# Two small fp32 matmuls per image split into column halves, and fewer small VectorE operations

## The chip, the cores and the metric

One core of a Trainium2 chip runs the kernel. The metric is the time of one execution on the device in microseconds (us), the median of the runs shown.

## What is computed

The input `x` is 16 images of 32 channels and 96 x 96 points in fp32. Each channel of each image is normalised by itself (32 groups of one channel), then goes through two 3 x 3 convolutions whose kernels are mixed for each image out of seven experts:

```
n      = (x - mean) / sqrt(var + 1e-5)                 per image and channel
pooled = n.mean over the image
gate   = softmax(pooled @ gate_w.T + gate_b)           7 numbers per image
kw1, kb1 = gate-weighted experts + conv1;  kw2, kb2 = the same for conv2
out1   = relu(conv3x3(n, kw1) + kb1)
out2   = conv3x3(out1, kw2) + kb2
result = x + (n + out2)
```

## The kernel before, in words

**Layout.** The 128 partitions hold 4 neighbouring image rows x 32 channels; 24 such bands (25 for the hidden image, which is shifted by one row) lie along the free dimension. A matmul contracts over all 128 partitions (4 rows x 32 channels) and gives 64 columns (2 output rows x 32 channels), for one of three horizontal taps. Rows 1 and 2 of four come from the tile itself ("straight": `a1`, `a2`), the other two from a copy whose partition halves are exchanged and shifted ("crossed": `c1`, `c2`). So each tap is a pair of 128*64 matmuls, one side to PSUM partitions 0 to 63, the other to 64 to 127 (L376). fp16 high and low parts of image and kernel are multiplied in three products; a convolution is 5 groups of 9 pairs, and an image is 90 pairs.

**The order of work.** Every engine runs a list written out by hand, `slot(s)`, for s = 1, 2, ... In slot s TensorE does conv1 of image s and conv2 of image s-1, with two small fp32 matmuls for image s+2 between the groups: `gather_rows` (L359) sums the channel statistics over the four partitions of a channel, `logits` (L367) sums the gate's products over the partitions. Both were one matmul over 128 columns. VectorE does in slot s: the statistics of image s+2 (L601) and `aggregate` (L606 to L608), which prepares the operand of `gather_rows`; `channel_moments` (L616 to L619), which reads the result; the seven steps of `mixture` for image s+1 (L646); `biases` (L656, L657) and `weights` (L663); the low part of the hidden image, `hidden_low` (L677); the rim of the hidden image, `clear_rim` (L684); and `finish` (L693). GpSimd turns the variance into the coefficients (`coefficients`, L846 to L856), forms the low part of the next image (L865) and adds the residual (`residual`, L879). ScalarE normalises (L491, L496), evacuates conv1 (L534), rounds the kernels (L519), copies `a2` into `c2` (`cross2`, L550) and takes exponentials. SyncE's queue loads images (L260), stores results (L274), and makes the crossed copies of the image (L287) and of the kernels (`cross_weights`, L296).

**What ties them together.** conv1 of image s+1 begins with a wait for that image's crossed kernels (`w_crossed`), so after `weights`. VectorE's `channel_moments` stands ahead of six of the seven `mixture` steps and waits for `gather_rows`, which TensorE issues after the fourth group of conv1. `biases` stands ahead of `weights`.

**The rim.** The hidden image needs zero rows above and below. `clear_rim` was called twice per image, after groups 0 and 4 (partitions 64 to 95 of band 0, partitions 96 to 127 of band 24), each with a wait for the low part just written; `cross2` waits for the first of the two before its second half, conv2 for both.

Of the kernel before, what the change touches and what calls it, by code (L numbers as in the profile page):

```python
# [29 lines left out]
F32 = mybir.dt.float32  # L30
# [5 lines left out]
P = 128  # L36
EPS = 1e-5

WS = 16.0
# [51 lines left out]
def build(nc, x, w1, b1, w2, b2, ew1, eb1, ew2, eb2, gw, gb, out):  # L91
# [18 lines left out]
    with ctx:  # L110
# [27 lines left out]
        row = sb("row", [P, 2, G])  # L138
# [3 lines left out]
        minus_half = sb("minus_half", [P, 1])  # L142

# [7 lines left out]
        NUMBER, VEPS, NMEAN, RSTD, NBIAS, RS1, RB, B1, POOLED, NMAX, ESUM, RSUM, MEAN, VAR, SCALED, B2 = range(16)  # L151
# [168 lines left out]
        def _(pe):  # L320
# [35 lines left out]
            def gather_rows(t):  # L356

                pe.wait_ge(mv_ok, t.number + 1)
                nc.tensor.matmul(pstat[:, 0:3 * G], same[:, :],  # L359
                                 triples[t.parity][:, :, :].rearrange("p g a -> p (g a)"),  # L360
                                 start=True, stop=True).then_inc(rows_ps, 1)

            def logits(t):
                pe.wait_ge(gwp_ok, t.number + 1)
                if not t.known(0):
                    pe.wait_ge(logit_ok, t.number)
                nc.tensor.matmul(pgate[:, 0:E], ones[:, :], gwp[t.ring][:, :],  # L367
                                 start=True, stop=True).then_inc(gate_ps, 1)
# [48 lines left out]
            def conv2_group(s, g):  # L417
                if g == 0:

                    pe.wait_ge(lo2_ok, (s.number + 1) * GRP)  # L420
                    pe.wait_ge(crossed2, s.number + 1)
                    pe.wait_ge(rim_ok, 2 * (s.number + 1))

                if s.at_least(N - 1):
                    pe.wait_ge(fin_ok, (s.number - 1) * GRP + g + 1)
                else:
                    pe.wait_ge(hid_ok, (s.number + 1) * GRP + g + 1)
                n = min(SPG, NB - g * SPG)
                products(1, s, g, PRODUCTS,
                      (CROSSED, c2[s.parity], g * SPG, n, 0),  # L430
                      (STRAIGHT, a2[s.parity], g * SPG + 1, n, 0)).then_inc(conv2_ps, 1)
# [36 lines left out]
        def _(act):  # L468
# [70 lines left out]
            def cross2(t, half):  # L539


                if half == 1:
                    act.wait_ge(rim_ok, 2 * t.number + 1)
                else:
                    act.wait_ge(lo2_ok, (t.number + 1) * GRP)
                    if t.at_least(2):
                        act.wait_ge(conv2_ps, (t.number - 1) * GRP)
                d, a = (halves(k[t.parity])[half].rearrange("p a b w -> p a (b w)").bitcast(F32) for k in (c2, a2))
                first = (1 - half) * RP // 2
                last = nc.scalar.copy(d, a[:, :, first:first + NB * RP // 2])  # L550
                if half == 1:
                    last.then_inc(crossed2, 1)
# [34 lines left out]
        def _(dve):  # L587
# [16 lines left out]
            def aggregate(t):  # L604

                link(nc.vector.bn_aggr(mv[t.ring][:, :], stats[t.ring][:, :, :].rearrange("p a b -> p (a b)")))  # L606
                nc.vector.tensor_scalar(triples[t.parity][:, :, 1], row[:, 0, :], mv[t.ring][:, 0:1], None, ALU.mult)
                nc.vector.tensor_scalar(triples[t.parity][:, :, 2], row[:, 1, :], mv[t.ring][:, 1:2], None,  # L608
                                        ALU.mult).then_inc(mv_ok, 1)

            def channel_moments(t):
# [4 lines left out]
                nc.vector.tensor_copy(c[:, NUMBER:NUMBER + 1], pstat[:, 0:1])  # L616
                link(nc.vector.bn_aggr(c[:, MEAN:VAR + 1], pstat[:, 0:3 * G]))
                nc.vector.tensor_scalar(c[:, NMEAN:NMEAN + 1], c[:, MEAN:MEAN + 1], -1.0, None, ALU.mult)
# [32 lines left out]
            def biases(t):  # L651
# [3 lines left out]
                mixed = mix[:, E % 2, :, TAPS:TAPS + 1]  # L655
                nc.vector.tensor_scalar(c[:, B1:B1 + 1], mixed[:, 0, :], HS / WS, None, ALU.mult)  # L656
                nc.vector.tensor_scalar(c[:, B2:B2 + 1], mixed[:, 1, :], 1.0 / WS, None, ALU.mult).then_inc(bias_ok, 1)  # L657
# [22 lines left out]
            def clear_rim(s, g):  # L680

                dve.wait_ge(lo2_ok, s.number * GRP + g + 1)
                p0, j = (P - 2 * C, 0) if g == 0 else (P - C, NS - 1)
                nc.vector.memset(a2[s.parity][p0:p0 + C, :, j, 1:1 + W], 0.0).then_inc(rim_ok, 1)  # L684
# [26 lines left out]
            def row_constants():  # L711
# [5 lines left out]
                link(nc.vector.tensor_reduce(row[:, 0, :], ident[:, :].rearrange("p (g c) -> p g c", g=G), AX_X, ALU.add))  # L717
                link(nc.vector.tensor_scalar(row[:, 1, :], row[:, 0, :], float(PIX), None, ALU.mult))
                for i in range(2):
                    last = nc.vector.tensor_copy(triples[i][:, :, 0], row[:, 1, :])  # L720
# [58 lines left out]
            clear_rim(Sample(0, 0), 0)  # L779
# [4 lines left out]
            clear_rim(Sample(0, 0), GRP - 1)  # L784
# [3 lines left out]
            def slot(s):  # L788
# [4 lines left out]
                run(clear_rim, s, 0, 0, 0)  # L793
# [15 lines left out]
                run(clear_rim, s, 0, 0, GRP - 1)  # L809
# [10 lines left out]
        def _(pool):  # L820
            link = Link(pool, pool_link)
            nc.gpsimd.memset(minus_half[:, :], -0.5)

# [12 lines left out]

            for straight, shifted in ((a1, c1), (a2, a2)):
# [5 lines left out]
            def coefficients(t):  # L843
# [3 lines left out]
                nc.gpsimd.tensor_tensor(c[:, NBIAS:NBIAS + 1], c[:, NMEAN:NMEAN + 1], c[:, RSTD:RSTD + 1],  # L847
                                        ALU.mult).then_inc(coef_ok, 1)
# [70 lines left out]
```

## Time and profile before

| | |
|---|---|
| median of 3 runs | 365.44 us (365.11 to 365.81) |
| the profiled execution | 366.37 us, of which the span of the trace is 364.6 us |
| busy: PE, VectorE, ScalarE, GpSimd | 317.4, 288.0, 252.8, 192.9 us |

The span runs from the first to the last instruction of the trace; the time of an execution includes some microseconds around it. Busy shares are averages over the start (until about 69 us), the steady slots (to about 303 us) and the end, in which only TensorE has much to do.

### The profile page before, as it was taken

How to read it: one execution, taken by the hardware profiler on the slowest of the kernel's cores; microseconds unless marked ns; L12 is line 12 of the kernel's file. 1: busy time of each engine (PE TensorE's matmuls, PEld its weight loads, DVE VectorE, ACT ScalarE, POOL GpSimd, SP SyncE). 2: the span in 40 equal slices, each digit the busy share in tenths (PEclk: the TensorE clock that was granted, in tenths of full speed). 3: DMA queues.
4: the chain of work that ended last, by engine and by line, in shares of the span. 5: the costliest groups of instructions: out<-in, count | busy, mean ns of one | idle time of the engine just before them, and what ended most of it. 6: DMA issues, size and time to landing. Idle time of an engine off the chain costs nothing.

```text
span 364.6 us, 7708 instructions
## 1 busy us (share of the span) xinstructions
PE 317.4 (87%) x2983; PEld 200.6 (55%) x2983; DVE 288.0 (79%) x651; ACT 252.8 (69%) x278; POOL 192.9 (53%) x236
## 2 busy tenths in 40 slices
PE   2327664499999999999899989999999999999994
PEld 2216432257565656565566646575756565676552
DVE  4699945698989989898979896989989898693432
ACT  1155219896878778787869695878887797965710
POOL 8039517492838475665739391848475656921000
PEclk9999989599999999999999999999999999999999
DMA  9932930599989797989997899979898977575055
GB/s 197 222 70 57 227 77 3 120 167 202 210 186 211 177 216 179 211 174 205 191 217 145 201 199 220 173 180 219 186 211 188 211 173 151 122 174 142 0 131 130
DMA packets 109379, 60.86 MB, mean 167 GB/s; under 512 B 102944, under 2 KB 105248, under 8 KB 109344
## 3 DMA queue, kind: packets, MB, share of 16 engines
q1 hardware_dynamic: 108544, 59.79, 78.9%
q10 hardware_dynamic: 608, 0.59, 0.6%
q8 instruction: 23, 0.38, 0.5%
q14 instruction: 12, 0.10, 0.1%
q0 software_dynamic: 192, 0.01, 0.0%
HBM read 19.47 MB, written 18.87 MB: 105 GB/s over the span
## 4 chain that ended last, share of the span: by engine, by line
PE 60%; DVE 19%; DMA 10%; SPq 3%; ACT 3%; POOL 2%; issue 2%; ACTq 0%; DVEq 0%; POOLq 0%
PE pg L376 56%; DVE mix L646 9%; DMA wts<-wts 7%; DVE a L677 3%; DVE wts L663 3%; DMA c<-a 2%; PE pg L339 2%; DVE stats L601 2%; PE pstat L359 2%; POOL a L865 1%; SPq L260 1%; DMA natural<-in_L_conv_conv_w 1%; SPq L296 1%; SPq L287 1%; ACT xh L491 1%
## 5 line engine op out<-in xcount | busy, mean ns | idle before, releaser
L376 PE MATMUL pg<-a,wts 128*64 128x480 f16 (+1 forms) x1440 | 292.2, 362 | 11.3 <-DMA c<-a 6.3
L376 PE MATMUL pg<-c,wts 128*64 128x480 f16 (+1 forms) x1440 | 297.7, 366 | 0.0
L376 PEld LDWEIGHTS pg<-c,wts 128*64 128x64 f16 x1440 | 154.5, 110 | 72.2 <-issue 1.1
L376 PEld LDWEIGHTS pg<-a,wts 128*64 128x64 f16 x1440 | 154.8, 110 | 43.3 <-issue 8.7
L865 POOL TENSOR_TENSOR a<-xh,a 128x576 f16<-128x576 f32 x64 | 79.1, 1268 | 13.4 <-POOL col L873 9.3
L534 ACT ACTIVATE hid<-pg,col 128x480 f32<-128x480 f32 x80 | 52.5, 657 | 46.7 <-PE pg L376 37.1
L646 DVE SCALAR_TENSOR_TENSOR mix<-bank,gate,mix 128x386 f32<-128x386 f32 x96 | 73.9, 770 | 2.4
L846 POOL TENSOR_TENSOR col<-col,minus_half 128x1 f32<-128x1 f32 x16 | 13.5, 841 | 111.6 <-DVE col L619 111.6
L550 ACT COPY c<-a 64x2352 f32<-64x2352 f32 x32 | 68.9, 2152 | 2.1 <-DVE a L677 1.9
L677 DVE TENSOR_TENSOR a<-hid,a 128x480 f16<-128x480 f32 x80 | 52.5, 657 | 21.2 <-ACT a L534 20.9
L693 DVE SCALAR_TENSOR_TENSOR img<-pg,img 128x480 f32<-128x480 f32 (+1 forms) x80 | 48.2, 632 | 13.6 <-PE pg L376 13.1
L879 POOL TENSOR_SCALAR img<-img,col 128x1152 f32<-128x1152 f32 x32 | 57.9, 1817 | 0.1
L534 ACT ACTIVATE a<-pg,col 128x480 f16<-128x480 f32 x80 | 52.5, 656 | 0.0
L601 DVE BATCH_NORM_STATS2 stats<-img 128x6 f32<-128x384 f32 x96 | 45.6, 544 | 0.1
L491 ACT ACTIVATE xh<-img,col 128x2304 f32<-128x2304 f32 x16 | 36.9, 2306 | 11.3 <-POOL col L847 11.3
L496 ACT ACTIVATE a<-img,col 128x2304 f16<-128x2304 f32 (+1 forms) x17 | 37.3, 2194 | 6.5 <-POOL col L847 6.5
L663 DVE TENSOR_TENSOR wts<-mix,wts 128x384 f16<-128x384 f32 x16 | 20.6, 1288 | 0.3 <-ACT wts L519 0.3
L359 PE MATMUL pstat<-triples,same 128*128 128x12 f32 x32 | 7.0, 293 | 15.4 <-DVE triples L608 15.4
L519 ACT CAST wts<-mix 128x384 f16<-128x384 f32 x16 | 8.2, 512 | 15.9 <-DVE mix L646 15.9
L359 PEld LDWEIGHTS pstat<-triples,same 128*128 128x128 f32 x32 | 5.5, 215 | 21.4 <-DVE triples L608 16.0
L616 DVE COPY col<-pstat 128x1 f32<-128x1 f32 x16 | 2.5, 157 | 18.6 <-PE pstat L359 18.6
L339 PE MATMUL pg<-ident,padded 128*128 128x128 f32 x24 | 5.6, 424 | 8.4 <-DVE padded L707 8.4
(61 smaller groups left out, 143.4 us busy)
## 6 DMA issues: line engine op xcount, KB each, us to landing
c<-a SPq DMA_DIRECT2D x28, 588.0 KB, 7.0
img<-in_x SPq DMA_DIRECT2D x56, 288.0 KB, 7.0
out<-img SPq DMA_DIRECT2D x60, 180.0 KB, 3.0
out<-img SPq DMA_DIRECT2D x60, 108.0 KB, 2.6
wts<-wts SPq DMA_DIRECT2D x28, 96.0 KB, 2.5
c<-a SPq DMA_DIRECT2D x8, 294.0 KB, 5.9
img<-in_x SPq DMA_DIRECT2D x16, 144.0 KB, 5.0
out<-img SPq DMA_DIRECT2D x4, 120.0 KB, 2.1
```

The costliest lines, as they stand in the source:

```text
L376: last = nc.tensor.matmul(pg[g][side * 64:side * 64 + 64, at:at + nb * W].rearrange("p (b w) -> p b w", w=W), wts[s.c % WSETS][kind][:, v, ...
L491: nc.scalar.activation(xh[t.parity][:, :, :], img[t.ring][:, :, :], ACT.Identity, bias=c[:, NBIAS:NBIAS + 1], scale=c[:, RSTD:RSTD + 1]).t ...
L496: return nc.scalar.activation(a1[t.parity][:, HI, b0:b1, 1:1 + W], img[t.ring][:, b0:b1, :], ACT.Identity, bias=c[:, NBIAS:NBIAS + 1], sca ...
L534: last = nc.scalar.activation(o, pg[g][:, 0:SPG * W].rearrange("p (b w) -> p b w", w=W), ACT.Relu, bias=c[:, B1:B1 + 1], scale=HS / WS)
L550: last = nc.scalar.copy(d, a[:, :, first:first + NB * RP // 2])
L601: last = nc.vector.bn_stats(stats[t.ring][:, j, :], flat[:, j * SC:(j + 1) * SC])
L646: nc.vector.scalar_tensor_tensor(out=mix[:, (e + 1) % 2, :, :], in0=bank[:, e, :, :], scalar=gate[t.ring][:, e:e + 1], in1=bank[:, E, :, : ...
L663: nc.vector.tensor_tensor(st[:, :, LO, :], mix[:, E % 2, :, 0:TAPS], st[:, :, HI, :], ALU.subtract).then_inc(w_ok, 1)
L677: nc.vector.tensor_tensor(a2[s.parity][:, LO, j0:j1, 1:1 + W], hid[g_parity(s, g)][:, :, :], a2[s.parity][:, HI, j0:j1, 1:1 + W], ALU.subt ...
L693: nc.vector.scalar_tensor_tensor(out=r, in0=pg[g][:, 0:(b1 - b0) * W].rearrange("p (b w) -> p b w", w=W), scalar=1.0 / (WS * HS), in1=r, o ...
L865: last = nc.gpsimd.tensor_tensor(a1[t.parity][:, LO, b0:b1, 1:1 + W], xh[t.parity][:, b0:b1, :], a1[t.parity][:, HI, b0:b1, 1:1 + W], ALU. ...
L879: last = nc.gpsimd.tensor_scalar(img[t.ring][:, b0:b1, :], img[t.ring][:, b0:b1, :], c[:, RS1:RS1 + 1], c[:, RB:RB + 1], ALU.mult, ALU.add)
```

## The change

1. `gather_rows` and `logits` issue two fp32 matmuls of 64 columns each in place of one of 128 columns. The semaphore is raised by the second.
2. `aggregate`: one `tensor_tensor` with a broadcast pair in place of two `tensor_scalar`.
3. `channel_moments`: a copy of a number that nothing reads (L616) and the negated mean (L618) are gone; GpSimd negates in the instruction that forms the bias of the normalisation.
4. `biases`: one `tensor_tensor` with a constant pair in place of two `tensor_scalar`.
5. `clear_rim` is called once per image. The zero row of band 0 is written into both `c2` buffers once at the start by GpSimd, and `cross2` leaves that piece alone, which makes three copies of two.

```
-                nc.tensor.matmul(pstat[:, 0:3 * G], same[:, :],
-                                 triples[t.parity][:, :, :].rearrange("p g a -> p (g a)"),
-                                 start=True, stop=True).then_inc(rows_ps, 1)
+                for h0, h1 in ((0, P // 2), (P // 2, P)):
+                    last = nc.tensor.matmul(pstat[h0:h1, 0:3 * G], same[:, h0:h1],
+                                            triples[t.parity][:, :, :].rearrange("p g a -> p (g a)"),
+                                            start=True, stop=True)
+                last.then_inc(rows_ps, 1)
...
-                nc.tensor.matmul(pgate[:, 0:E], ones[:, :], gwp[t.ring][:, :],
-                                 start=True, stop=True).then_inc(gate_ps, 1)
+                for h0, h1 in ((0, P // 2), (P // 2, P)):
+                    last = nc.tensor.matmul(pgate[h0:h1, 0:E], ones[:, h0:h1], gwp[t.ring][:, :],
+                                            start=True, stop=True)
+                last.then_inc(gate_ps, 1)
...
-                    pe.wait_ge(rim_ok, 2 * (s.number + 1))
+                    pe.wait_ge(rim_ok, s.number + 1)
...
-                if half == 1:
-                    act.wait_ge(rim_ok, 2 * t.number + 1)
-                else:
+                def copy(p0, p1, b0, b1, first):
+                    d, a = (k[t.parity][p0:p1, :, :, :].rearrange("p a b w -> p a (b w)").bitcast(F32) for k in (c2, a2))
+                    r = RP // 2
+                    return nc.scalar.copy(d[:, :, b0 * r:b1 * r], a[:, :, (b0 + first) * r:(b1 + first) * r])
+                if half == 0:
                     act.wait_ge(lo2_ok, (t.number + 1) * GRP)
...
+                    copy(0, P // 2, 0, NB, 1)
+                else:
+                    copy(P - C, P, 0, 1, 0)
+                    copy(P // 2, P, 1, NB, 0).then_inc(crossed2, 1)
...
-                nc.vector.tensor_scalar(triples[t.parity][:, :, 1], row[:, 0, :], mv[t.ring][:, 0:1], None, ALU.mult)
-                nc.vector.tensor_scalar(triples[t.parity][:, :, 2], row[:, 1, :], mv[t.ring][:, 1:2], None,
-                                        ALU.mult).then_inc(mv_ok, 1)
+                pair = mv[t.ring][:, :].rearrange("p (o a) -> p o a", o=1).to_broadcast([P, G, 2])
+                nc.vector.tensor_tensor(triples[t.parity][:, :, 1:3], row[:, :, :], pair, ALU.mult).then_inc(mv_ok, 1)
...
-                nc.vector.tensor_copy(c[:, NUMBER:NUMBER + 1], pstat[:, 0:1])
                 link(nc.vector.bn_aggr(c[:, MEAN:VAR + 1], pstat[:, 0:3 * G]))
-                nc.vector.tensor_scalar(c[:, NMEAN:NMEAN + 1], c[:, MEAN:MEAN + 1], -1.0, None, ALU.mult)
...
-                mixed = mix[:, E % 2, :, TAPS:TAPS + 1]
-                nc.vector.tensor_scalar(c[:, B1:B1 + 1], mixed[:, 0, :], HS / WS, None, ALU.mult)
-                nc.vector.tensor_scalar(c[:, B2:B2 + 1], mixed[:, 1, :], 1.0 / WS, None, ALU.mult).then_inc(bias_ok, 1)
+                nc.vector.tensor_tensor(c[:, B1:B2 + 1], mix[:, E % 2, :, TAPS], bias_scales[:, :],
+                                        ALU.mult).then_inc(bias_ok, 1)
...
-            def clear_rim(s, g):
+            def clear_rim(s):
-                dve.wait_ge(lo2_ok, s.number * GRP + g + 1)
-                p0, j = (P - 2 * C, 0) if g == 0 else (P - C, NS - 1)
-                nc.vector.memset(a2[s.parity][p0:p0 + C, :, j, 1:1 + W], 0.0).then_inc(rim_ok, 1)
+                dve.wait_ge(lo2_ok, (s.number + 1) * GRP)
+                nc.vector.memset(a2[s.parity][P - C:P, :, NS - 1, 1:1 + W], 0.0).then_inc(rim_ok, 1)
...
+            nc.gpsimd.memset(bias_scales[:, 0:1], HS / WS)
+            nc.gpsimd.memset(bias_scales[:, 1:2], 1.0 / WS)
...
+            pool.wait_ge(ident_ok, 1)
+            for i in range(2):
+                link(nc.gpsimd.memset(c2[i][P // 2:P - C, :, 0, :], 0.0))
...
-                nc.gpsimd.tensor_tensor(c[:, NBIAS:NBIAS + 1], c[:, NMEAN:NMEAN + 1], c[:, RSTD:RSTD + 1],
-                                        ALU.mult).then_inc(coef_ok, 1)
+                nc.gpsimd.tensor_scalar(c[:, NBIAS:NBIAS + 1], c[:, MEAN:MEAN + 1], c[:, RSTD:RSTD + 1], -1.0,
+                                        ALU.mult, ALU.mult).then_inc(coef_ok, 1)
```

How this stands in the order of VectorE's instructions, in a steady slot from the low part of group 0 to the moments of the channels, before:

```order
L677 TENSOR_TENSOR a_0<-hid,a_0 128x5x96
L606 BN_AGGR mv<-stats 128x2
L607 TENSOR_SCALAR triples<-row,mv 128x4
L608 TENSOR_SCALAR triples<-row,mv 128x4
L684 MEMSET a_0 32x2x96
L635 RECIPROCAL col<-col 128x1
L636 TENSOR_SCALAR gate<-expo,col 128x7
L646 SCALAR_TENSOR_TENSOR mix<-bank,gate 128x386
L677 TENSOR_TENSOR a_0<-hid,a_0 128x5x96
L616 COPY col<-pstat 128x1
L617 BN_AGGR col<-pstat 128x2
L618 TENSOR_SCALAR col<-col 128x1
```

and now (the lines are those of the changed file):

```order
L679 TENSOR_TENSOR a_0<-hid,a_0 128x5x96
L612 BN_AGGR mv<-stats 128x2
L614 TENSOR_TENSOR triples<-row,mv 128x4x2
L638 RECIPROCAL col<-col 128x1
L639 TENSOR_SCALAR gate<-expo,col 128x7
L649 SCALAR_TENSOR_TENSOR mix<-bank,gate 128x386
L679 TENSOR_TENSOR a_0<-hid,a_0 128x5x96
L621 BN_AGGR col<-pstat 128x2
L622 TENSOR_SCALAR col<-col 128x1
```

Four instructions are gone from this stretch (one of the pair that fills `triples`, the first memset, the copy and the negation); a fifth goes later in the slot, where `biases` stands.

ScalarE's order at the end of a slot, where `c2` is made, before:

```order
L519 CAST wts_0<-mix 128x2x192
L496 ACTIVATE a_1<-img,col 128x24x96
L550 COPY c_1<-a_1 64x2352 x2
L510 ACTIVATE expo,col<-logit,col 128x7
L534 ACTIVATE hid<-pg,col 128x480
```

and now:

```order
L549 COPY c_1<-a_1 64x2352
L549 COPY c_1<-a_1 32x2x49
L549 COPY c_1<-a_1 64x2x1127
L515 ACTIVATE expo,col<-logit,col 128x7
L539 ACTIVATE hid<-pg,col 128x480
```

The second copy has become a small one (32 partitions, one band) and one over 23 bands in place of 24.

## Rows read from the trace of the kernel before

**Rows 1.** The page: busy time, share of the span, instructions
```profile
PE 317.4 (87%) x2983; PEld 200.6 (55%) x2983; DVE 288.0 (79%) x651; ACT 252.8 (69%) x278; POOL 192.9 (53%) x236
```
**Rows 2.** Timeline, PE: the gathers (start us, us); intervals of slots, and one wait
```profile
89.56 0.39 PE L359 MATMUL pstat<-triples,same 128*128 128x12 f32 x2
...
187.09 0.39 PE L359 MATMUL pstat<-triples,same 128*128 128x12 f32 x2
...
205.97 0.39 PE L359 MATMUL pstat<-triples,same 128*128 128x12 f32 x2
...
302.96 0.39 PE L359 MATMUL pstat<-triples,same 128*128 128x12 f32 x2
```
**Rows 3.** Waits: waiter <- waited for: us in total, times, longest us
```profile
PEld pg L376 <- DMA wts<-wts: 7.3, 8, 2.2
PEld pgate L367 <- issue: 5.4, 14, 0.4
PEld pstat L359 <- issue: 5.4, 13, 0.8
```
**Rows 4.** Timeline, PE and PEld around one gather
```profile
166.26 0.57 PE L376 MATMUL pg<-c,wts 128*64 128x480 f16 x2
166.76 0.39 PE L359 MATMUL pstat<-triples,same 128*128 128x12 f32 x2
...
167.08 0.39 PE L376 MATMUL pg<-c,wts 128*64 128x480 f16 x1
...
166.76 0.30 PEld L359 LDWEIGHTS pstat<-triples,same 128*128 128x128 f32 x2 [0.39 <-issue]
```
**Rows 5.** Chain of waits, 160 to 180 us: start us, us, what
```profile
174.91 0.52 SPq L296
...
175.47 4.11 DMA wts<-wts
```
**Rows 6.** Timeline, VectorE, same slot
```profile
163.60 0.23 DVE L607 TENSOR_SCALAR triples<-row,mv 128x4 f32<-128x4 f32 x1
...
164.30 0.16 DVE L635 RECIPROCAL col<-col 128x1 f32<-128x1 f32 x1
...
167.19 0.16 DVE L616 COPY col<-pstat 128x1 f32<-128x1 f32 x1 [1.23 <-PE pstat L359]
167.26 0.20 DVE L617 BATCH_NORM_AGGREGATE col<-pstat 128x2 f32<-128x12 f32 x1
167.50 0.15 DVE L618 TENSOR_SCALAR col<-col 128x1 f32<-128x1 f32 x1
167.57 0.14 DVE L619 TENSOR_SCALAR col<-col 128x1 f32<-128x1 f32 x1
...
173.37 0.14 DVE L657 TENSOR_SCALAR col<-mix 128x1 f32<-128x1 f32 x1
173.43 1.45 DVE L663 TENSOR_TENSOR wts<-mix,wts 128x384 f16<-128x384 f32 x1
```
**Rows 7.** Timeline, GpSimd; L663 and L296: duration ns min/median/max; landings
```profile
170.71 3.77 POOL L879 TENSOR_SCALAR img<-img,col 128x1152 f32<-128x1152 f32 x2
L663 DVE TENSOR_TENSOR wts<-mix,wts x16: 548/1450/1452, 29.8 to 325.9; 128x384 f16<-128x384 f32 x16
DMA to landing us min/median/max: 2.1/2.5/4.6
```
**Rows 8.** Busy by stretches: length, PE, PEld, DVE, ACT, POOL; clock, DMA share, GB/s
```profile
187.20:206.00 18.80, 18.80 (x185) 11.85 (x185) 17.25 (x39) 15.60 (x17) 11.74 (x13) 1.00 0.84 179
206.00:226.90 20.90, 19.10 (x186) 11.87 (x185) 17.24 (x39) 15.60 (x17) 11.75 (x13) 1.00 1.01 208
```
**Rows 9.** Chain of waits, start of the kernel
```profile
53.63 0.22 DVE a L684
...
61.34 2.03 ACT c L550
```
**Rows 10.** Groups by line: busy us, mean ns of one | idle before
```profile
L510 ACT ACTIVATE expo<-logit,col 128x7 f32<-128x7 f32 x16 | 4.8, 300 | 2.1 <-DVE col L628 1.8
```

More of the change, by code:

```diff
@@ L137, in build @@
         same = sb("same", [P, P])
-        row = sb("row", [P, 2, G])
+        row = sb("row", [P, G, 2])
         triples = [sb(f"triples{i}", [P, G, 3]) for i in range(2)]
@@ L142, in build @@
         minus_half = sb("minus_half", [P, 1])
+        bias_scales = sb("bias_scales", [P, 2])
         stats = [sb(f"stats{i}", [P, STAT, 6]) for i in range(RING)]
@@ L150, in build @@
         gate = [sb(f"gate{i}", [P, E]) for i in range(RING)]
-        NUMBER, VEPS, NMEAN, RSTD, NBIAS, RS1, RB, B1, POOLED, NMAX, ESUM, RSUM, MEAN, VAR, SCALED, B2 = range(16)
+        VEPS, RSTD, NBIAS, RS1, RB, B1, B2, POOLED, NMAX, ESUM, RSUM, MEAN, VAR, SCALED = range(14)
         pg = [ctx.enter_context(nc.psum_tensor(f"pg{i}", [P, 512], F32)) for i in range(GRP)]
@@ L547, in cross2 @@
                         act.wait_ge(conv2_ps, (t.number - 1) * GRP)
[L548 to L552, printed above, removed]
+                    copy(0, P // 2, 0, NB, 1)
+                else:
+                    copy(P - C, P, 0, 1, 0)
+                    copy(P // 2, P, 1, NB, 0).then_inc(crossed2, 1)
             load_kernels()
@@ L716, in row_constants @@
                     nc.vector.tensor_copy(same[:, g * C:(g + 1) * C], pick[:, :])
-                link(nc.vector.tensor_reduce(row[:, 0, :], ident[:, :].rearrange("p (g c) -> p g c", g=G), AX_X, ALU.add))
-                link(nc.vector.tensor_scalar(row[:, 1, :], row[:, 0, :], float(PIX), None, ALU.mult))
+                link(nc.vector.tensor_reduce(row[:, :, 0], ident[:, :].rearrange("p (g c) -> p g c", g=G), AX_X, ALU.add))
+                link(nc.vector.tensor_scalar(row[:, :, 1], row[:, :, 0], float(PIX), None, ALU.mult))
                 for i in range(2):
-                    last = nc.vector.tensor_copy(triples[i][:, :, 0], row[:, 1, :])
+                    last = nc.vector.tensor_copy(triples[i][:, :, 0], row[:, :, 1])
                 link(last)
@@ L778, in _ @@
             channel_moments(Sample(0, 2))
-            clear_rim(Sample(0, 0), 0)
             hidden_low(Sample(0, 0), 1)
@@ L783, in _ @@
             hidden_low(Sample(0, 0), 4)
-            clear_rim(Sample(0, 0), GRP - 1)
+            clear_rim(Sample(0, 0))
             statistics(Sample(0, 3))
@@ L792, in slot @@
                 run(aggregate, s, 2, 2)
-                run(clear_rim, s, 0, 0, 0)
                 run(softmax_out, s, 1, 1)
@@ L808, in slot @@
                 run(hidden_low, s, 0, 0, 4)
-                run(clear_rim, s, 0, 0, GRP - 1)
+                run(clear_rim, s, 0, 0)
                 run(finish, s, -1, 0, 0)
```

## The prediction

> **What bounds the kernel now.** I read the page first: TensorE is busy 87% of the span, VectorE 79% [rows 1]. Neither share says what the next microsecond waits for, so I then took the timeline of TensorE and measured from one `gather_rows` to the next. The 11 intervals from 89.56 to 302.96 us make 213.4 us, 19.40 on average [rows 2]. Four of them are 18.9, such as 187.09 to 205.97 [rows 2]: that is TensorE with nothing to wait for. Eleven of these would be 207.7, so 5.7 us are waits. The list of waits names them: the weight loads of L376 wait 7.3 us in 8 places for the crossed kernels' DMA [rows 3].
>
> So two loops of nearly one length bound a slot, and the longer one wins:
> - **TensorE's own work**, 18.88 us.
> - **The loop of the kernels**: gather, VectorE's moments, six mixture steps, `biases`, `weights`, the DMA, conv1 of the next image, the next gather. In the slot shown the gather starts at 166.76 [rows 4], VectorE goes on at 167.19 [rows 6], SyncE issues the crossing at 174.91, its second DMA starts at 175.47 and takes 4.11 [rows 5]; conv1 begins and its next gather starts at 187.09 [rows 2]. Without the DMA d that is 187.09 - 166.76 - 4.11 = 16.22. The loop is 16.22 + d and wins if d is over 2.66. The landings are 2.1 at least, 2.5 in the middle, 4.6 at most [rows 7], which is why some slots wait and others don't.
>
> **The split matmuls.** Around a gather the last convolution matmul starts at about 166.46 (two starts in 0.57 us, each some 0.37 long) [rows 4]. Pairs follow each other every 0.204 us, so the next was due at 166.66; it starts at 167.08 [rows 4]. One small fp32 matmul thus costs TensorE 0.42 us: 0.10 before it starts (its load has 0.39 idle before it [rows 4], and both kinds together 10.8 us in 27 places [rows 3]) and 0.32 for two passes about 0.11 apart and the restart. It is the only instruction in the stream that takes 128 columns. Once it has the width of its neighbours, I expect the pause ahead of it to go. Against this stand four passes in place of two. Upper bound of a gain: passes of half the width take half of 0.11 and the two halves run side by side as the convolution's sides do, 0.11 in all, gain 0.31. Lower bound: four full passes (0.44), the pause (0.10) and the restart (0.10) stay, 0.64, a loss of 0.22. I take a cost of 0.17 and a gain of **0.25**, nearer the upper end, since rows 4 show two 64-column matmuls of the convolution going without any pause. Two per slot: 0.50.
>
> The Trainium skill (TensorEngine Tiling (Array Packing), Key Properties) says that changing the tiling mode drains the engine; the 0.39 idle is consistent with it. The same page (Instruction Overhead) gives a matmul some 60 cycles however short it is, which speaks against more passes: an estimate from it is 25 ns for each of four passes, 0.10 in all, and a gain of 0.32, 0.14 more per slot than the 0.50 that the sum takes. No row here shows that floor.
>
> **VectorE, on the loop.** Gone are L616 and L618. From the starts, L616 to L617 is 0.07 and L618 to L619 0.07 [rows 6]; together 0.14. `biases` becomes one instruction, worth 0.06 (L657 to L663 [rows 6]). But L663 takes 1.45 here and 0.55 at its fastest [rows 7], beside GpSimd's residual, which runs from 170.71 for 3.77 us [rows 7]: VectorE's instruction with two tensor inputs seems to wait for GpSimd. The new `biases` also has two tensor inputs and stands right ahead of it; it may wait in its place, and then the 0.06 is lost, and another 0.07 with it. I take 0 (between -0.07 and +0.06). GpSimd's new two-step negation: between 0 and 0.05 (one step of `tensor_scalar` against `tensor_tensor` there), beside VectorE's mixture; I take 0. The result reaches VectorE 0.43 after the gather's start; with the pause gone but more passes behind, between 0.1 sooner and 0.2 later; I take 0. The loop becomes 16.08 + d.
>
> **VectorE, off the loop.** From L607 to L635 there are 0.70 us [rows 6]: three instructions and a wait, where one stays. That gains 0.35 to 0.5 of VectorE's time, but VectorE then waits 1.23 for the gather [rows 6]. In steady slots it is worth nothing.
>
> **ScalarE** gets a third copy: at most the 0.30 of its smallest instruction [rows 10], less 0.08 for the shorter one. It is busy 15.6 of 18.8 us [rows 8] and conv2 needs `c2` some 9 us after it is made; hidden. GpSimd's two memsets at the start run while it waits for VectorE: nothing.
>
> **The sum**, against the profiled execution's 366.37 us:
> - Start, before 69 us: no slot runs yet and VectorE is in the chain. The pairs and the copies save about 0.4 ahead of image 0's low part; L616, L618 and the memset with its wait (0.07 + 0.07 + 0.33, of which the memset's 0.22 stands in the chain [rows 9]) save 0.47; the next `aggregate` 0.13; the added copy takes back 0.2, since L550 is in the chain here [rows 9]. **-0.8**.
> - First full slot, bound by TensorE: **-0.5**.
> - Four free intervals fall from 18.88 to the longer of 18.38 and 16.08 + 2.4: about 0.4 each, **-1.6**.
> - Seven waiting intervals gain what the loop gains, 0.14, a little more where the longer pause lets the loads drain: 0.15 each, **-1.05**.
> - End: one gather and one `logits` of TensorE's own work: **-0.4**.
>
> Together -4.35, so 362.0 for that execution. It lies 0.93 above the median of the runs (365.44), so the prediction for the median is **361.1**.
>
> **The rivals.**
> 1. *The DMA takes it back.* In the slot with the long crossing the DMA engines are busy for all of it (share 1.01), in the free one 0.84 [rows 8]. Shorter slots leave less room, and d could grow by what TensorE gains; or the split buys nothing because the pause stays. Then the start, the end and a little remain: 365.44 - 0.8 - 0.5 - 7 x 0.1 = 363.4. Against it: loads and crossing keep their distance, since both follow TensorE.
> 2. *Slower: the split costs more than it saves.* Place: between group 3 of conv1 and group 4, and in conv2. At the lower bound each call costs 0.22 more: 4 x 0.44 in free slots, 7 x (0.22 + 0.22 later result - 0.14) in waiting ones, 0.44 + 0.44 at the ends, less 0.8: +3.9, so 369.0. It decides from about 0.08 more per call.
> 3. *Slower: the new `biases` queues behind GpSimd by itself*, and L663 again: another 0.9 (1.45 - 0.55) in the loop, less 0.14; free slots have 0.26 to spare. About 11 x 0.55 less 1.7, +4: 369.8. The Trainium skill (GPSIMD Engine Reference, Key points) says that the two engines contend when VectorE has two SBUF inputs. Against it: GpSimd's residual has two parts only, and one mixture step and L663 already take one each.
> 4. *Much better.* `biases` in its one step gets in ahead of GpSimd's second part, or the crossing lands within 2.3 us in most slots. Then all slots are TensorE's 18.38: 213.4 - 202.2 = 11.2 less, with start and ends 1.7: 352.5. A part of it, 357, is likelier.
>
> **Chances.** Forecast 0.57 (its own range 359.5 to 362.8, from a gain of 0.17 to 0.31 per split and the bounds above); rival 1 0.20; rival 4 0.12; rivals 2 and 3 0.11 together. The range 357.0 to 364.6 leaves out rivals 2 and 3 and half of 4. A measurement of this kernel tells 0.2% (0.7 us) from no change: faster 0.84, same 0.06, slower 0.10.
>
> **What the profile after would show.** PEld's "issue" idle before the two small matmuls (10.8 us) gone; a free interval of about 18.4; VectorE 0.07 earlier at each removed instruction; L616 and L618 gone, and the waits for the crossed kernels in more slots, since TensorE's part of the race shrank more than the loop's. I am wrong if the small matmuls still have a pause before them, if the free interval is not under 18.7, or if the new `biases` takes about 1 us and L663 still 1.4.

## The result, and the profile after

The changed kernel took 358.4 us in the median of four runs (357.09 to 359.55), where 361.1 was predicted; the ratio to the kernel before is 0.9753 (95% interval 0.971 to 0.9795). It is faster, as forecast, but by 2.5% where 1.2% was expected. Here and below a ratio is taken over the executions within 1.5% of a kernel's fastest, a median over all of them. The profiled execution took 357.09 us, its span is 355.1 us, 9.5 less than before. The page of the changed kernel, first part:

```profile
PE 308.5 (87%) x3047; PEld 218.8 (62%) x3047; DVE 269.6 (76%) x571; ACT 254.0 (72%) x294; POOL 204.7 (58%) x240
```

These answer to [rows 1]. GpSimd is 12 us busier although it got only four memsets at the start (240 instructions in place of 236) and the negation inside an instruction that it already had; that is the first sign of what the prediction missed.

**Slots.** The changed kernel's timeline of TensorE, the two halves of a gather, at three successive slots (columns: start us, us):

```profile
105.68 0.23 PE L361 MATMUL pstat<-triples,same 128*64 128x12 f32 x2
106.04 0.23 PE L361 MATMUL pstat<-triples,same 128*64 128x12 f32 x2
...
123.49 0.23 PE L361 MATMUL pstat<-triples,same 128*64 128x12 f32 x2
124.22 0.23 PE L361 MATMUL pstat<-triples,same 128*64 128x12 f32 x2
...
143.35 0.23 PE L361 MATMUL pstat<-triples,same 128*64 128x12 f32 x2
143.72 0.23 PE L361 MATMUL pstat<-triples,same 128*64 128x12 f32 x2
```

The later half marks the slot, since the result is complete with it: 106.04, 124.22, 143.72, so 18.18 us for a free slot (18.88 before, 18.38 forecast) and 19.50 for one that waits. From the gather that was at 89.56 before to the last [rows 2], 11 intervals now make 294.15 - 87.02 = 207.13 us, 6.3 less than the 213.4 of before; 11 free ones would be 200.0, so 7.1 us are waits, more than the 5.7 of before.

**Around the small matmul.** The same timeline at the second of these gathers, PE:

```profile
123.41 0.36 PE L381 MATMUL pg<-c,wts 128*64 128x480 f16 x1
123.49 0.23 PE L361 MATMUL pstat<-triples,same 128*64 128x12 f32 x2
123.61 0.57 PE L381 MATMUL pg<-c,wts 128*64 128x480 f16 x2
123.82 0.39 PE L381 MATMUL pg<-a,wts 128*64 128x480 f16 x1
...
124.22 0.23 PE L361 MATMUL pstat<-triples,same 128*64 128x12 f32 x2
...
124.31 0.37 PE L381 MATMUL pg<-c,wts 128*64 128x480 f16 x1
```

The rows before showed a standstill of 0.42 us [rows 4]. Now one half goes at 123.49, while the other side of the array still works on the convolution, and the second half 0.73 us later. The two sides do not stop together as before. By the difference of the free slots, (18.88 - 18.18) / 2, a small matmul costs 0.35 less than the 0.42 of before, so some 0.07 us. The timeline has 0.09 for the side of the second half (`c`, from 124.22 to 124.31). The side of the first half goes on only 0.33 after it, at 123.82, and the slot is a free one all the same; what that side waits for isn't shown.

**Waits** of the changed kernel that answer to [rows 3] (us in total, times, longest):

```profile
DVE col L621 <- PE pstat L361: 22.2, 14, 4.0
PEld pg L381 <- DMA wts<-wts: 8.5, 7, 2.0
PEld pstat L361 <- issue: 0.2, 1, 0.2
```

Of the 10.8 us of "issue" before the small matmuls 0.2 are left. The first line is VectorE waiting for the gathers, 18.6 us before.

**VectorE's stretch of the loop**, the changed kernel's timeline, to be read against [rows 6]:

```profile
124.49 0.22 DVE L621 BATCH_NORM_AGGREGATE col<-pstat 128x2 f32<-128x12 f32 x1 [1.40 <-PE pstat L361]
124.74 0.15 DVE L622 TENSOR_SCALAR col<-col 128x1 f32<-128x1 f32 x1
124.81 1.93 DVE L649 SCALAR_TENSOR_TENSOR mix<-bank,gate,mix 128x386 f32<-128x386 f32 x3
126.66 0.66 DVE L679 TENSOR_TENSOR a<-hid,a 128x480 f16<-128x480 f32 x1
127.22 1.93 DVE L649 SCALAR_TENSOR_TENSOR mix<-bank,gate,mix 128x386 f32<-128x386 f32 x3
129.07 0.65 DVE L679 TENSOR_TENSOR a<-hid,a 128x480 f16<-128x480 f32 x1
129.64 1.10 DVE L658 TENSOR_TENSOR col<-mix,bias_scales 128x2 f32<-128x2 f32 x1
130.66 0.55 DVE L665 TENSOR_TENSOR wts<-mix,wts 128x384 f16<-128x384 f32 x1
```

SyncE issues the crossing at 131.24, 6.75 us after the result is read. Before, it was 174.91 - 167.19 = 7.72 [rows 5, 6]. The stretch is 0.97 shorter, where I had forecast 0.14. `biases` now takes 1.10 us and `weights` only 0.55 (1.45 before [rows 6]), as one of my bounds had it. But the last three mixture steps, 1.93 together, hold no long one any more, and that is new. The kernel before, timeline of VectorE and then of GpSimd, in the slot of [rows 6]:

```profile
170.04 2.77 DVE L646 SCALAR_TENSOR_TENSOR mix<-bank,gate,mix 128x386 f32<-128x386 f32 x3
...
168.93 0.22 POOL L849 TENSOR_SCALAR col<-col 128x1 f32<-128x1 f32 x1
```

GpSimd in the slot shown of the changed kernel:

```profile
124.97 0.88 POOL L850 TENSOR_TENSOR col<-col,minus_half 128x1 f32<-128x1 f32 x1 [5.19 <-DVE col L622]
125.96 0.26 POOL L851 TENSOR_SCALAR col<-col 128x1 f32<-128x1 f32 x1
126.19 0.64 POOL L853 TENSOR_SCALAR col<-col 128x1 f32<-128x1 f32 x1
126.79 0.57 POOL L854 TENSOR_TENSOR col<-mv,col 128x1 f32<-128x1 f32 x1
...
128.55 4.33 POOL L883 TENSOR_SCALAR img<-img,col 128x1152 f32<-128x1152 f32 x2
```

L883, the residual, starts 4.06 us after the moments were begun; before, L879 at 170.71 [rows 7] started 3.45 after L617 at 167.26 [rows 6]. GpSimd is later, and VectorE is faster for it. `hidden_low` (L679) also has two tensor inputs, but keeps its 0.65 us beside the residual (129.07) as elsewhere, so not every such instruction is held.

**The crossing.** The changed kernel's chain of waits in that slot (start us, us, what), against [rows 5]:

```profile
131.24 0.97 SPq L297
132.25 4.05 DMA wts<-wts
136.35 7.18 PE pg L381 x70
```

and its view of line L297:

```profile
DMA to landing us min/median/max: 2.1/3.2/4.9
```

The median time to land went from 2.5 [rows 7] to 3.2 us.

### The profile page after: what moved, and what is told of

The parts are those of the page before. It is cut to its first block, busy times and chain, and to the rows that moved or that the text cites. A ratio compares the mean times of both kernels' runs of the same rounds, so it can differ in the third digit from the quotient of the medians.

```text
span 355.1 us, 7776 instructions
## 1 busy us (share of the span) xinstructions
PE 308.5 (87%) x3047; PEld 218.8 (62%) x3047; DVE 269.6 (76%) x571; ACT 254.0 (72%) x294; POOL 204.7 (58%) x240
## 3 DMA queue, kind: packets, MB, share of 16 engines
HBM read 19.47 MB, written 18.87 MB: 108 GB/s over the span
## 4 chain that ended last, share of the span: by engine, by line
PE 66%; DVE 18%; DMA 8%; ACT 3%; issue 3%; SPq 1%; ACTq 0%; DVEq 0%
PE pg L381 63%; DVE mix L649 7%; DMA wts<-wts 7%; DVE a L679 2%; DVE col L658 2%; PE pg L340 2%; DVE stats L607 2%; DMA natural<-in_L_conv_conv_w 1%; DVE wts L665 1%; SPq L297 1%; DVE wts L672 1%; PE pstat L361 1%; ACT xh L496 1%; ACT c L549 1%; ACT a L501 1%
## 5 line engine op out<-in xcount | busy, mean ns | idle before, releaser
L381 PE MATMUL pg<-a,wts 128*64 128x480 f16 (+1 forms) x1440 | 291.9, 363 | 11.5 <-DMA wts<-wts 6.1
L381 PE MATMUL pg<-c,wts 128*64 128x480 f16 (+1 forms) x1440 | 292.4, 367 | 0.0
L381 PEld LDWEIGHTS pg<-c,wts 128*64 128x64 f16 x1440 | 154.3, 110 | 49.4 <-issue 0.9
L381 PEld LDWEIGHTS pg<-a,wts 128*64 128x64 f16 x1440 | 155.0, 110 | 46.6 <-DMA wts<-wts 8.5
L549 ACT COPY c<-a 64x2352 f32<-64x2352 f32 (+2 forms) x48 | 71.9, 1497 | 2.3 <-DVE a L679 1.9
L679 DVE TENSOR_TENSOR a<-hid,a 128x480 f16<-128x480 f32 x80 | 53.1, 665 | 22.6 <-ACT a L539 22.4
L649 DVE SCALAR_TENSOR_TENSOR mix<-bank,gate,mix 128x386 f32<-128x386 f32 x96 | 62.9, 655 | 2.4
L883 POOL TENSOR_SCALAR img<-img,col 128x1152 f32<-128x1152 f32 x32 | 64.6, 2025 | 0.1
L621 DVE BATCH_NORM_AGGREGATE col<-pstat 128x2 f32<-128x12 f32 x16 | 3.4, 216 | 22.2 <-PE pstat L361 22.2
L361 PE MATMUL pstat<-triples,same 128*64 128x12 f32 x64 | 7.4, 209 | 14.2 <-DVE triples L614 14.2
L361 PEld LDWEIGHTS pstat<-triples,same 128*64 128x64 f32 x64 | 8.1, 154 | 16.4 <-DVE triples L614 14.8
L658 DVE TENSOR_TENSOR col<-mix,bias_scales 128x2 f32<-128x2 f32 x16 | 15.9, 992 | 0.1
L371 PEld LDWEIGHTS pgate<-gwp,ones 128*64 128x64 f32 x64 | 7.9, 144 | 9.3 <-POOL gwp L860 7.4
```

Source lines behind the costliest of these rows:

```text
L381: last = nc.tensor.matmul(pg[g][side * 64:side * 64 + 64, at:at + nb * W].rearrange("p (b w) -> p b w", w=W), wts[s.c % WSETS][kind][:, v, ...
L549: return nc.scalar.copy(d[:, :, b0 * r:b1 * r], a[:, :, (b0 + first) * r:(b1 + first) * r])
L649: nc.vector.scalar_tensor_tensor(out=mix[:, (e + 1) % 2, :, :], in0=bank[:, e, :, :], scalar=gate[t.ring][:, e:e + 1], in1=bank[:, E, :, : ...
L658: nc.vector.tensor_tensor(c[:, B1:B2 + 1], mix[:, E % 2, :, TAPS], bias_scales[:, :], ALU.mult).then_inc(bias_ok, 1)
L679: nc.vector.tensor_tensor(a2[s.parity][:, LO, j0:j1, 1:1 + W], hid[g_parity(s, g)][:, :, :], a2[s.parity][:, HI, j0:j1, 1:1 + W], ALU.subt ...
L883: last = nc.gpsimd.tensor_scalar(img[t.ring][:, b0:b1, :], img[t.ring][:, b0:b1, :], c[:, RS1:RS1 + 1], c[:, RB:RB + 1], ALU.mult, ALU.add)
```

## The experiments

Theory A: the change holds two separate gains, the split (TensorE's own period and an earlier result) and a shift of GpSimd's instructions against VectorE's; the crossing DMA takes part of both back. Theory B: the split is behind all of it. All times below are medians of runs made beside the kernel before on the same chip; "stretch" is the time from the reading of the moments (L617 before, L621 in the changed kernel) to the issue of the crossing, 7.65 in the kernel before, which is the 7.72 less the removed copy's 0.07, and 6.75 in the changed one. The kernel before had a median of 366.9 beside e1 to e4, 367.1 beside e5 to e8 and 368.4 beside e9 to e12; so ratios are compared rather than times.

### One piece again (e1_unsplit)

```diff
-                for h0, h1 in ((0, P // 2), (P // 2, P)):
-                    last = nc.tensor.matmul(pstat[h0:h1, 0:3 * G], same[:, h0:h1], ...
+                nc.tensor.matmul(pstat[:, 0:3 * G], same[:, :], ...
```

and the same in `logits`. Expected:

> The changed kernel with both small fp32 matmuls in one piece of 128 columns again; all else of the change stays. Theory A (two separate gains: the split shortens TensorE's own period and hands the result over earlier, and a shift of GpSimd's work frees VectorE from one of two collisions): VectorE's stretch from the moments of a slot to the issue of the crossing stays at about 6.75 us, a free slot goes back to 18.88 us, few slots wait for the crossed kernels; about 361 us. Theory B (everything comes from the split, the shorter VectorE stretch too): the stretch is 7.6 us again, 364 us.

Measured: 362.2 us, ratio 0.9861 (0.9806 to 0.9916). The stretch is 6.74, 8 of the 11 intervals are 18.87 or 18.88, and TensorE's weight loads wait for the crossing in three places, 2.3 us in all. Theory A holds: the shorter stretch has nothing to do with the split.

### The split alone (e2_split_only)

The kernel before with the split matmuls of the change and nothing else. Expected:

> The kernel before with nothing but the two small matmuls split. Theory A: a free slot takes 18.2 us, the result reaches VectorE 0.25 us earlier, VectorE's stretch stays 7.7 us and more slots wait for the crossing; about 361.5 us. Theory B: the stretch falls to about 6.8 as well and the time is within 1 us of the changed kernel, 358.5 us.

Measured: ten executions spread from 361.1 to 371.9 us, median 367.0 where theory A had 361.5; ratio 0.9886 (0.9835 to 0.9937). The profiled execution took 367.2 us. The stretch is 7.65. Slots of 18.2 to 18.6 us alternate with slots of 19.9 to 22.3. Its waits (same columns as above):

```profile
PEld pg L380 <- DMA wts<-wts: 15.8, 9, 3.0
```

TensorE's own period fell by 0.70 as in the changed kernel, and the wait for the crossing rose from 7.3 [rows 3] to 15.8 us. By itself the split is worth half of the change's gain or nothing. The loop of the kernels has not got shorter with it, so that the wait grows; e3, which has the same stretch and the same waits, agrees. The two slots of over 22 us hold something else besides, TensorE's clock, which is shown under e3.

### The negation back on VectorE (e3_negation_back)

The changed kernel with

```diff
+                nc.vector.tensor_scalar(c[:, NMEAN:NMEAN + 1], c[:, MEAN:MEAN + 1], -1.0, None, ALU.mult)
...
-                nc.gpsimd.tensor_scalar(c[:, NBIAS:NBIAS + 1], c[:, MEAN:MEAN + 1], c[:, RSTD:RSTD + 1], -1.0,
-                                        ALU.mult, ALU.mult).then_inc(coef_ok, 1)
+                nc.gpsimd.tensor_tensor(c[:, NBIAS:NBIAS + 1], c[:, NMEAN:NMEAN + 1], c[:, RSTD:RSTD + 1],
+                                        ALU.mult).then_inc(coef_ok, 1)
```

Expected:

> The changed kernel with the negated mean made by VectorE again and GpSimd's plain product in place of its two-step one. Theory A (GpSimd's instruction after it just misses the boundary between two mixture steps because the two-step form is some 0.05 us longer, and everything behind it on GpSimd shifts by 0.6 us): GpSimd's residual starts 3.1 us after the first mixture step again in place of 3.7, the last mixture step takes 1.4 us again, VectorE's stretch is 7.6 us in place of 6.75; 360.5 us. Rival C (the added instruction costs only its 0.07 us): residual at 3.7, stretch 6.8, 358.6 us.

Measured: ten executions, one of 836.7 us and the others from 363.7 to 372.1, median 368.5; ratio 0.9995 (0.9947 to 1.0043). One instruction of 0.07 us on VectorE, back in its place with the plain product on GpSimd, takes away the whole gain of the change. Timeline of this kernel, VectorE, then GpSimd:

```profile
110.88 2.77 DVE L650 SCALAR_TENSOR_TENSOR mix<-bank,gate,mix 128x386 f32<-128x386 f32 x3
...
114.14 0.15 DVE L659 TENSOR_TENSOR col<-mix,bias_scales 128x2 f32<-128x2 f32 x1
114.23 1.49 DVE L666 TENSOR_TENSOR wts<-mix,wts 128x384 f16<-128x384 f32 x1
```

```profile
109.59 0.20 POOL L852 TENSOR_TENSOR col<-col 128x1 f32<-128x1 f32 x1
109.77 0.22 POOL L854 TENSOR_SCALAR col<-col 128x1 f32<-128x1 f32 x1
109.95 0.49 POOL L855 TENSOR_TENSOR col<-mv,col 128x1 f32<-128x1 f32 x1
...
111.55 3.76 POOL L884 TENSOR_SCALAR img<-img,col 128x1152 f32<-128x1152 f32 x2
```

The moments are read at 108.09, so the residual starts 3.46 after them and the stretch is 7.65, as before the change. The small GpSimd instruction L854 takes 0.22 here and 0.64 in the changed kernel (L853 there). The mixture's steps begin at 108.47 and follow each other by 0.65: here L854 starts at 109.77, 1.30 after the first, at the seam between the second and third step; in the changed kernel it starts 126.19 - 124.81 = 1.38 after, has missed the seam, and lasts until the next one (126.83 against 126.74, the end of the third). What I had put down as "0 to 0.05 us" of GpSimd's new form decides by these hundredths over 0.6 us of GpSimd's time and 0.84 of VectorE's. The pair of `biases` (L659) isn't held here, 0.15 us, and `weights` is, 1.49: which of the two it is also hangs on where GpSimd stands.

The marks of theory A are all there, but its time of 360.5 us isn't. Waits for the crossing are 15.0 us in 8 places, much as in e2, and part of the rest is the clock. Two slots of this kernel by stretches (length, PE, PEld, VectorE, ScalarE, GpSimd busy; clock, DMA share, GB/s):

```profile
165.00:187.50 22.50, 20.06 (x194) 13.89 (x191) 16.79 (x35) 15.80 (x18) 11.75 (x13) 0.92 1.04 216
246.00:266.50 20.50, 18.34 (x192) 14.28 (x190) 16.70 (x35) 15.79 (x18) 11.74 (x13) 1.00 1.02 212
```

In the first, TensorE's granted clock fell from 2.4 to 1.2 GHz (0.51 from 179 us on, 1.00 again by 183) after the weight loads had waited 2.8 us for the crossing, and TensorE is busy 1.7 us longer for about as many matmuls. It happens in two of the five slots with a wait of over 2 us here, and in two of five in e2's profile (the slots of 22.2 and 22.3 us); the longest such wait of the kernel before is 2.2 us [rows 3], and its clock stays at 1.00 through the slots. That the wide spread of e2 and e3 comes from this is likely, but not shown, since one trace of each was kept.

### The negation alone (e4_negation_only)

The kernel before with L618 gone and GpSimd's two-step form, nothing else. Expected:

> The kernel before with nothing but the negation moved into GpSimd's instruction. Theory A: the residual starts at 3.7 us after the first mixture step, the last mixture step takes 0.6 us in place of 1.46, VectorE's stretch is 6.8 us in place of 7.72, nearly all slots run at TensorE's 18.88 us; 361 us. Rival C: only 0.07 us of the stretch goes, 365 us.

Measured: 362.4 us, ratio 0.9857 (0.9802 to 0.9912). Residual 4.05 after the moments, stretch 6.66. This part alone gives about half of the gain (0.0143 of 0.0247, or of the 0.0299 that the changed kernel had when it was run again), as does all of the change without the split (0.9861).

### Work added, nothing removed (e6_small_op_added)

The kernel before with

```diff
+                nc.gpsimd.tensor_scalar(spare[:, :], c[:, RSTD:RSTD + 1], 1.0, None, ALU.add)
                 nc.gpsimd.tensor_scalar(c[:, RS1:RS1 + 1], c[:, RSTD:RSTD + 1], 1.0, None, ALU.add)
```

Expected:

> The kernel before with one more small GpSimd instruction (a 128 x 1 tensor_scalar into a spare tile) in the coefficients of each image; nothing is taken away. Theory A (GpSimd's place among VectorE's instructions decides): what follows misses a boundary of the mixture steps, the residual starts 4.1 us after the moments in place of 3.45, the last mixture step takes 0.6 us in place of 1.46 and the stretch from the moments to the issue of the crossing is 6.8 us in place of 7.65: faster by 3 to 4 us, 362 us, although work was only added. Rival D (the shorter stretch came from the instructions that VectorE no longer has): stretch 7.65, 366 us.

Measured: 361.6 us, ratio 0.9859 (0.9822 to 0.9896). Its GpSimd and its VectorE:

```profile
130.32 0.22 POOL L850 TENSOR_SCALAR spare<-col 128x1 f32<-128x1 f32 x1
130.51 0.51 POOL L851 TENSOR_SCALAR col<-col 128x1 f32<-128x1 f32 x1
...
132.76 4.25 POOL L881 TENSOR_SCALAR img<-img,col 128x1152 f32<-128x1152 f32 x2
```

```profile
131.43 1.93 DVE L647 SCALAR_TENSOR_TENSOR mix<-bank,gate,mix 128x386 f32<-128x386 f32 x3
```

The added instruction takes the seam, the next waits for the following one, the residual starts 4.11 after the moments (128.65), and no mixture step is held. So the gain is not the removed instruction's: 16 needless instructions make the kernel before 1.4% faster.

### `biases` in two instructions again (e7_biases_back)

```diff
-                nc.vector.tensor_tensor(c[:, B1:B2 + 1], mix[:, E % 2, :, TAPS], bias_scales[:, :],
-                                        ALU.mult).then_inc(bias_ok, 1)
+                nc.vector.tensor_scalar(c[:, B1:B1 + 1], mixed[:, 0, :], HS / WS, None, ALU.mult)
+                nc.vector.tensor_scalar(c[:, B2:B2 + 1], mixed[:, 1, :], 1.0 / WS, None, ALU.mult).then_inc(bias_ok, 1)
```

Expected:

> The changed kernel with `biases` as two tensor_scalar again. Theory A: VectorE waits for GpSimd's residual once in either form, at `biases` (1.1 us) with the pair and at `weights` (1.45 us) without; the stretch is 6.75 us within 0.1 and the time that of the changed kernel, 358 us. Rival: the pair of inputs is what costs, and the stretch gets 0.5 us shorter or more, 356 us.

Measured: 356.3 us, ratio 0.9717 (0.9674 to 0.976); the changed kernel has 0.9753 and, run again, 0.9701, so the times do not tell the two apart. The profiles do: the stretch is 6.67 against 6.75 (`weights` takes 1.04 here after 0.25 of waiting for ScalarE, where I had expected 1.45), and at the start of the kernel `biases` of image 0 stands beside GpSimd's low part. Changed kernel, then this one, VectorE:

```profile
28.27 1.25 DVE L658 TENSOR_TENSOR col<-mix,bias_scales 128x2 f32<-128x2 f32 x1
29.45 0.15 DVE L628 SCALAR_TENSOR_TENSOR logit<-pgate,gbias 128x7 f32<-128x7 f32 x1
```

```profile
28.26 0.15 DVE L659 TENSOR_SCALAR col<-mix 128x1 f32<-128x1 f32 x1
28.33 0.14 DVE L660 TENSOR_SCALAR col<-mix 128x1 f32<-128x1 f32 x1
```

The pair takes 1.25 us there, the two single ones 0.29; behind them ScalarE's exponential of image 1 starts at 29.18 in place of 29.83. Whether this edit of the change costs more than it saves these times can't tell; e10 below can.

### The crossed copies by VectorE (e5_copy_on_vector)

The changed kernel without `cross_weights` in SyncE's list and with

```diff
                 run(weights, s, 1, 1)
+                run(cross_early, s, 1, 1)
```

Expected:

> The changed kernel with the crossed copy of each image's kernels made by two VectorE copies right behind `weights` in place of two DMAs. If the DMA's time to land (3 to 5 us in every second slot) is what holds the changed kernel back, the waits for the crossed kernels go and every slot takes TensorE's own 18.2 us: 11 intervals 200 us in place of 207, 351 us. If VectorE, which gains 0.8 to 1.7 us of work per slot on 16.7, becomes the bound, intervals are 18.4 to 19 and the time is 353 to 358. If the DMA was not the brake, 358 us as the changed kernel.

Measured: 359.1 us, ratio 0.9791 (0.9752 to 0.983), no faster than the changed kernel. All waits for the crossing are gone, and 12 others of 0.52 us have come, one in each slot: conv1 waits for `finish` on VectorE. Every interval is 18.9. Over 88 to 288 us VectorE is busy 194 of 200 us: it is the bound now, as the second of the expected cases said, though the time is 1 us above the 353 to 358 of that case.

### The copies shared (e8_copy_shared)

As e5, but ScalarE makes one of the two, behind its high part:

```diff
+                nc.scalar.copy(halves(cr)[1].rearrange("p v a b -> p (v a b)").bitcast(F32),
+                               halves(st)[0].rearrange("p v a b -> p (v a b)").bitcast(F32)).then_inc(w_crossed[t.ring], 16)
```

Expected:

> As the copies by VectorE, but one of the two is made by ScalarE behind its high part of the next image. Both engines have room (ScalarE 16 us of 18.2, VectorE 16.7), and the copies are done some 9.5 us after the gather where conv1 begins at 10.8: all slots 18.2 us, 351 us. If ScalarE's place in the order comes too late, conv1 waits in every slot and intervals are 18.5 to 19: 354 to 358 us.

Measured: 351.1 us, ratio 0.9565 (0.9535 to 0.9595). TensorE, by stretches (length, PE, PEld, VectorE, ScalarE, GpSimd busy; clock, DMA share, GB/s), waits for nothing:

```profile
88.00:180.00 92.00, 92.00 (x958) 65.44 (x954) 85.79 (x178) 80.40 (x96) 63.45 (x65) 1.00 0.94 194
180.00:288.00 108.00, 108.00 (x1120) 75.28 (x1117) 101.46 (x208) 96.06 (x114) 76.17 (x78) 1.00 0.97 200
```

So the crossing DMA took 5 to 7 us back from the change (0.9753 or, run again, 0.9701, less 0.9565, of 366). The DMA engines are as busy as before (0.94 to 0.97); they move images and results in time, and it is only the short transfer that conv1 stood waiting for that held it up.

### Four together (e9 to e12)

The changed kernel again, and three kernels that differ by one part from e8: `biases` in two, the small matmuls in one piece, and the shared copies in the kernel before.

> The changed kernel as it is, beside the three below. 358.4 us as before; stretch 6.75 us, every second slot waiting for the crossed kernels.

Measured: 357.3 us, ratio 0.9701 (0.9664 to 0.9737).

> The kernel with the crossed copies shared by VectorE and ScalarE, and `biases` as two tensor_scalar again. If a slot there is TensorE's own work, the form of `biases` is worth nothing any more: 351 us within 0.7. If VectorE was still close behind, 350 us or less.

Measured: 348.8 us, ratio 0.9471 (0.9435 to 0.9507), the fastest of all and clear of e8. The intervals are those of e8, 18.18; the gain lies at the start, where the moments of image 3 are read at 67.08 us in place of 68.77, with ScalarE's exponential of image 1 0.76 us earlier (29.12 against 29.88), as in e7. The rest of these 1.7 us lies in the wait for the DMA of the crossed image, and no run separates it. In all kernels with the split the moments of images 1 and 2 are 26.2 to 26.8 us apart with `biases` in two (e2, e7, e10) and 27.4 to 27.9 with the pair (the changed kernel, e3, e5, e8, e9). I had looked for a difference in the slots only.

> The shared copies with both small matmuls in one piece again. With no wait for a DMA the slots show the price of the 128-column form alone: 18.88 us in place of 18.18 in every slot, 0.70 x 11 intervals and 1 to 1.4 at the ends over the 351 us of the shared copies, 360 us.

Measured: 360.2 us, ratio 0.9772 (0.9736 to 0.9809). Every interval is 18.87 or 18.88. This is the price of the two 128-column matmuls with nothing else in the way: 0.70 in each of 11 intervals is 7.7 us, and the ratios of e11 and e8 differ by 0.0207 or 7.6 us. Its waits show them as before the change:

```profile
PEld pgate L367 <- issue: 5.4, 14, 0.4
PEld pstat L359 <- issue: 5.4, 13, 0.8
```

> The kernel before with the shared copies and nothing else. If the loop through the crossing DMA was all that held the kernel before over TensorE's 18.88 us, all intervals are 18.88 and 5.7 us go: 361 us. If VectorE, with 0.8 us more work in a slot than the changed kernel has, comes to bound it, intervals are 19 and more, 363 us.

Measured: 360.9 us, ratio 0.9805 (0.9767 to 0.9844), every interval 18.87 or 18.88. Beside e11 it shows that without the DMA in the loop all of the change but the split is worth nothing that these runs can tell (0.9772 and 0.9805, intervals that overlap): a shorter stretch only counts while the crossing is late.

## Why the prediction was right or wrong

**What bounds the kernel: right.** Two loops, TensorE's own work and the loop of the kernels through the crossing; e12 removed the second and all slots fell to 18.88.

**The split: right in kind, gain too small.** I took 0.25 us for each call; measured is (18.88 - 18.18) / 2 = 0.35, above my upper bound of 0.31. The bound assumed that both sides pause together for 0.11. They don't: each side takes its half in its own stream. The pause ahead came from the width, as I had guessed. The Trainium skill (TensorEngine Tiling (Array Packing), Key Properties) says that tiles operate independently and that changing the mode drains the engine; e11 and e8 agree with both, 0.42 against 0.07 us, though a drain as such is seen in no trace. Its 60 cycles for a short matmul (Instruction Overhead) gave an estimate of 0.10 us for four passes, and so 0.05 for the two that each side has; the 0.07 measured lies between.

**The result's latency: I had 0, and it stays open.** From the time when the next pair was due to the reading of the result it was 0.53 us (166.66 to 167.19 [rows 6]); from the later half to the reading it is now 124.49 - 124.22 = 0.27. But the later half itself starts 0.36 to 0.73 behind the first, and no run tells how much of that is in the loop.

**VectorE on the loop: this step failed.** The sum took 0.14 us off the loop of the kernels for VectorE, and the runs showed 0.97. The removed instructions are worth 0.14 as said. The other 0.84 is one mixture step that no longer waits for GpSimd's residual (2.77 for three steps before, 1.93 now). I had seen that VectorE's instructions with two inputs wait for GpSimd and applied it to `weights` and to the new `biases`, and I had put GpSimd's own delay, "between 0 and 0.05", at zero without asking what it would meet. The bound itself held: from L851 to L853 it is 0.23 us, from L847 to L849 before it was 0.18. e3, e4 and e6 show that those hundredths made about half of the change's gain, and that without them the rest of it came to nothing (e3). Rival 4 had the size of it but not the place.

**`biases`: the bound was right** for the slots (0.08 lost, of 0.07 allowed) and wrong in that I looked at them alone: at the start the same instruction takes 1.25 us.

**The DMA: what rival 1 feared came beside the forecast**, not in its place. Landing went from 2.5 to 3.2 us in the median and waits from 5.7 to 7.1 us; slots of 18.18 and of 19 to 20 alternate. My reason against it was that loads and crossing keep their distance. That a free slot brings the next crossing nearer to the loads of the last may be what is wrong with it, but the reason why landings got longer stays open: the median is 2.8 and 2.9 in e1 and e4, which have the short stretch without the split, and 2.6 in e2, which has the split without the short stretch.

**Slips in the prediction.** Rival 2's 3.9 us over 365.44 make 369.3, not 369.0. GpSimd got four memsets, not two. Neither changes the forecast.

**The sum.** By the moments' reading, the span before splits into 70.35 to the first steady slot, 233.12 for 12 intervals and 61.1 after them; the changed kernel has 68.52, 225.90 and 60.7. The start gave 1.8 (0.8 forecast), the slots 7.2 (3.15), the end 0.4 (0.4). Of the 1.8, 0.98 lie between the moments of images 2 and 3 (17.27 us before, 16.29 now). The kernels with neither the new `aggregate` nor the new rim (e2, e4, e6, e12) have 17.2 to 17.3 there, all the others 16.3 or 16.4, so it comes from one of these two edits; no run separates them.

## What to carry to other kernels

A matmul of another width in a stream of column tiles costs a standstill of both sides (0.42 us against 0.07); give it the width of its neighbours. Where two loops are nearly of one length, price a change against both, and then ask which wait is left: here the one small transfer in the loop was worth 5 to 7 us, half to three quarters of what the whole change gave. And where two engines take turns, as VectorE and GpSimd do here, look at the seams: which instruction of the one meets which of the other can outweigh what is removed, so profile each small edit by itself.

## What the runs showed of the hardware

- VectorE's mixture steps, `weights` and the pair of `biases`, all with two SBUF inputs, take turns with GpSimd: a GpSimd instruction that comes during a mixture step ends with it (L853 0.64 in place of 0.22), and the VectorE instruction behind can then wait for GpSimd (a mixture step 1.46 in place of 0.62, `weights` 1.45 in place of 0.55, a 128 x 2 product 1.10 us). `hidden_low`, also with two, keeps 0.65 us beside the residual; why is not shown. A `tensor_scalar` on one column isn't held (0.14 to 0.15 beside GpSimd's low part). The Trainium skill (GPSIMD Engine Reference, Key points) states the contention; that the order is settled at the seams between instructions, so that 0.08 us decide over 0.84, is what e3 and e6 add.
- The two 128*64 halves of a small fp32 matmul within a stream of 128*64 fp16 ones lengthen a slot by 0.07 us, and the sides may stand 0.36 to 0.73 us apart (105.68 and 106.04; 123.49 and 124.22). A matmul issued behind the second half can start ahead of it on the other side (L381 on `a` at 123.82, the half at 124.22).
- DMAs of 96 KB each took between 2.1 and 4.9 us to land in slots over which the DMA engines were 94 to 98% busy.
- TensorE's granted clock fell to 1.2 GHz for about 3.4 us after four of the ten waits of 2.2 to 3.0 us in e2 and e3, at 1.7 us of TensorE's time in the slot compared under e3.
